# Selective scan on one core: later step-input jobs, one sum moved to VectorE, sums of a section copied out a bank earlier and in runs of 16

## The reference, cut to what matters

```python
dt = softplus(dts + dt_proj_b)            # per direction and channel
def step(h, inp):
    dt_l, u_l, B_l, C_l = inp
    dA = jnp.exp(dt_l[..., None] * A)
    h = h * dA + (dt_l * u_l)[..., None] * B_l[:, :, None, :]
    y = jnp.einsum('bkdn,bkn->bkd', h, C_l)
    return (h, y)
```

## Time and profile before

| | us |
|---|---|
| median of 3 runs (10565.58 to 10573.44) | 10570.25 |
| profiled execution, its own time | 10566.93 |
| its span in the trace | 10565.1 |
| VectorE busy | 7070.9 |
| GpSimd busy | 4147.8 |
| TensorE busy | 8515.6 |
| ScalarE busy | 4478.1 |

### The profile page before, as it was taken

One profiled execution on the slowest core, in us unless ns is written; L12 is line 12 of the kernel. 1 busy time (PEld: TensorE's weight loads), 2 busy tenths in 40 slices (PEclk: granted clock), 3 DMA queues, 4 the chain that ended last, 5 costly groups with the idle time before them and its releaser, 6 DMA issues. The chain is left out here.

```text
span 10565.1 us, 129307 instructions
## 1 busy us (share of the span) xinstructions
PE 8515.6 (81%) x40748; PEld 6002.4 (57%) x40748; DVE 7070.9 (67%) x9395; ACT 4478.1 (42%) x8485; POOL 4147.8 (39%) x2787
## 2 busy tenths in 40 slices
PE   4777777777777778599999999958558988996657
PEld 2444344434444444399999999947334444443445
DVE  6999799979997999444444454432356766653446
ACT  4666566656665666322222222223214444443231
POOL 3999599959995999211111111000000000000001
PEclk8999899999998999799999999979759999997668
DMA  4555355535553555100000000031310000103000
GB/s 129 164 162 162 110 161 161 163 110 164 161 164 110 161 162 164 43 12 14 12 13 11 13 14 10 8 103 33 130 51 19 14 19 19 28 1 130 20 21 18
DMA packets 332596, 835.12 MB, mean 79 GB/s; under 512 B 35796, under 2 KB 111832, under 8 KB 318654
## 3 DMA queue, kind: packets, MB, share of 16 engines
q1 hardware_dynamic: 331910, 826.64, 25.4%
HBM read 758.85 MB, written 39.08 MB: 76 GB/s over the span
## 5 line engine op out<-in xcount | busy, mean ns | idle before, releaser
L754 POOL TENSOR_TENSOR ss_work<-ss_dtu,ss_ringb 128x768 f32<-128x768 f32 x1536 | 2755.3, 1817 | 251.8 <-POOLq L59 248.3
L618 PE MATMUL ss_ps<-ss_work,ss_ident 128*128 128x512 f32 (+1 forms) x6144 | 2276.7, 517 | 446.8 <-POOL ss_work L764 329.5
L618 PEld LDWEIGHTS ss_ps<-ss_work,ss_ident 128*128 128x128 f32 x6144 | 1221.4, 203 | 1221.8 <-issue 872.0
L738 DVE TENSOR_TENSOR_SCAN ss_work<-ss_ps,ss_last,ss_work 128x768 f32<-128x768 f32 x1024 | 1811.2, 1802 | 95.8 <-issue 42.4
L671 ACT ACTIVATE ss_ps<-ss_dt,ss_a_neg 128x768 f32<-128x768 f32 x1536 | 1376.0, 896 | 273.1 <-DVE ss_work L738 254.6
L1234 ACT ACTIVATE stu_XT<-cv_ps 128x384 fp32r<-128x384 f32 x768 | 377.1, 491 | 1789.3 <-DVE cv_ps L1281 1361.9
L723 DVE TENSOR_TENSOR ss_work<-ss_work,ss_ps 128x1152 f32<-128x1152 f32 x768 | 1019.7, 1328 | 1.2 <-ACT ss_ps L679 1.2
L2227 ACT ACTIVATE at_probs<-at_ps 128x768 f32<-128x768 f32 x864 | 694.6, 810 | 709.3 <-PE at_ps L2181 708.7
L2245 DVE TENSOR_REDUCE at_top<-at_ps 128x1 f32<-128x384 f32 x1728 | 878.8, 553 | 167.6 <-PE at_ps L2165 165.7
L1664 POOL MEMSET c_pooled<- 128x2048 f32 x2 | 3.6, 1808 | 2487.2 <-POOLq L59 2487.2
L738 DVE TENSOR_TENSOR_SCAN ss_work<-ss_ps,ss_work 128x768 f32<-128x768 f32 x512 | 879.5, 1744 | 66.3 <-issue 33.2
(11 more groups left out here) (543 smaller groups left out, 14912.5 us busy)
## 6 DMA issues: line engine op xcount, KB each, us to landing
ss_ringb<-scan_rows SPq DMA_DIRECT2D x768, 384.0 KB, 3.7
ss_ringc<-scan_rows SPq DMA_DIRECT2D x768, 384.0 KB, 3.8
c_w<-in_l_ffn_w SPq DMA_DIRECT2D x64, 1024.0 KB, 7.4
at_packs<-at_high SPq DMA_DIRECT2D x64, 288.0 KB, 5.5
cv_raw<-in_l_ffn_phi_odd SPq DMA_DIRECT2D x16, 576.5 KB, 3.6
cv_raw<-in_l_ffn_phi_even SPq DMA_DIRECT2D x16, 576.0 KB, 4.3
at_packs<-at_qk SPq DMA_DIRECT2D x32, 288.0 KB, 5.5
ff_weights<-in_l_conv_fw SPq DMA_DIRECT2D x10, 640.0 KB, 10.4
```

Source lines behind the costliest of these rows:

```text
L618: return pe.matmul(acc[:, d * WIN + a:d * WIN + e], ident[:, :], weighed[:, t % DEEP, d, a:e], start=n == 0 and e - a == 512, stop=n == NS ...
L738: dve.tensor_tensor_scan(hid[:, t % DEEP, d, ::step], decay[d][:, ::step], drive[:, t % DEEP, d, ::step], start, ALU.mult, ALU.add).then_i ...
L754: pool.tensor_tensor(drive[:, t % DEEP, d, :], dtu[:, t // NST % 2, d, :], ringb[:, t % RING, :], ALU.mult).then_inc(s["driven"], 1)
```

## The change

Input jobs run in states 4 to 9 and sum jobs in 10 to 14, which is one fewer. The sixth sum (half 1, last 256 columns) is made by VectorE in state 12 with both operands in SBUF, and a semaphore `sum_last` tells ScalarE and GpSimd. The Exp, Ln and `weigh_input` steps move back by one state, except GpSimd's second, which stays at 13. Since no job is left in state 3, TensorE issues none inside state 0. The old `y` is added in states 5 to 8. The first `summed` of a state is signalled after the first 256 columns of half 1, and `keep_sums` of half 0 waits for that one. For column windows `keep_sums` walks its operands in the other order: it writes 16 neighbouring elements at a time and reads PSUM with a step of 48.

```diff
-    INPUT_AT, SUM_AT = (3, 4, 5, 6, 7, 8), (9, 10, 11, 12, 13, 14)
+    INPUT_AT, SUM_AT = (4, 5, 6, 7, 8, 9), (10, 11, 12, 13, 14)
     JOBS = len(INPUT_AT) + len(SUM_AT)
-    EXP_AT, LOG_AT, READY_AT = (5, 8), (6, 9), (10, 13)
-    FIRST_Y, KEEP_AT = 3, (1, 2)
+    EXP_AT, LOG_AT, READY_AT, SUM_LAST_AT = (6, 9), (7, 10), (11, 13), 12
+    FIRST_Y, KEEP_AT = 5, (1, 2)
+    def kept_sums(i, d):
+
+        return kept_jobs(i, len(INPUT_AT) + min(PARTS * (d + 1), len(SUM_AT)))
...
-                if n != 1:
-                    beside(t + 2)
+                beside(t + 2)
...
                     add_weighed(t, 0, 0, 512)
-                    beside(t + 3)
                     if i:
                         pe.wait_ge(s["kept"], D2 * i)
...
-                add_weighed(t, 0, 512, WIN).then_inc(s["summed"], 1)
-                add_weighed(t, 1, 0, 256)
+                add_weighed(t, 0, 512, WIN)
+                add_weighed(t, 1, 0, 256).then_inc(s["summed"], 1)
                 add_weighed(t, 1, 256, WIN).then_inc(s["summed"], 1)
...
-                    act.wait_ge(s["z_kept"], kept_jobs(i, len(INPUT_AT) + PARTS * (d + 1)))
+                    act.wait_ge(s["z_kept"], kept_sums(i, d))
+                    if d:
+                        act.wait_ge(s["sum_last"], i)
...
-                act.wait_ge(s["summed"], 2 * NST * (i + 1))
-                act.activation(window(y[:, d, :], SECTIONS[i]), acc[:, d * WIN:(d + 1) * WIN].rearrange("p (a b) -> p a b", b=48), ACT.Copy).then_inc(s["kept"], 1)
+                act.wait_ge(s["summed"], 2 * NST * (i + 1) - 1 + d)
+                order = "p a b -> p a b" if SECTIONS[i][0] % 2 == 0 else "p a b -> p b a"
+                total = acc[:, d * WIN:(d + 1) * WIN].rearrange("p (a b) -> p a b", b=48)
+                act.activation(window(y[:, d, :], SECTIONS[i]).rearrange(order), total.rearrange(order), ACT.Copy).then_inc(s["kept"], 1)
...
                     if d == 0 and t:
                         weigh(t - 1)
+                    if d == 0 and n == SUM_LAST_AT and i + 1 < len(SECTIONS):
+                        dve.wait_ge(s["soft"], D2 * (i + 1) + 2)
+                        z = dt[:, (i + 1) % 2, 1, WIN - SIDE:WIN]
+                        dve.tensor_tensor(z, z, dtu[:, (i + 1) % 2, 1, WIN - SIDE:WIN], ALU.add).then_inc(s["sum_last"], 1)
...
-                pool.wait_ge(s["z_kept"], kept_jobs(i, len(INPUT_AT) + PARTS * (d + 1)))
+                pool.wait_ge(s["z_kept"], kept_sums(i, d))
+                if d:
+                    pool.wait_ge(s["sum_last"], i)
```

More of the change, by code:

```diff
@@ L300, in selective_scan_mixer @@
         s1 = Signals(nc, "ss1", "loaded framed projected padded cleared conv_own conv_done convolved gated zed zgated made even_kept odd_kept")
-        s2 = Signals(nc, "ss2", "b0 b1 b2 b3 c0 c1 c2 c3 first_stored even_stored odd_stored kept_x copied driven decayed scanned weighted pool_weighted ended summed kept z_full z_kept exponent soft added dt_ready")
+        s2 = Signals(nc, "ss2", "b0 b1 b2 b3 c0 c1 c2 c3 first_stored even_stored odd_stored kept_x copied driven decayed scanned weighted pool_weighted ended summed kept z_full z_kept sum_last exponent soft added dt_ready")
         s3 = Signals(nc, "ss3", "mean centred squared varied logged sd_ready normed gated summed added stored")
```

## The result

| | us | ratio to before (95%) |
|---|---|---|
| before, 9 runs | 10570.14 (10561.05 to 10580.5) | |
| changed, 9 runs | 10593.87 (10576.19 to 10606.2) | 1.0022 (1.0012 to 1.0033) |

The change makes the kernel 24 us slower (0.22%), about the smallest difference that these runs can tell from none; 49 us less were forecast, and the range ended at 10560. All medians here are of fast runs: one run of add_11 (11086 us, granted clock 0.75 where the others have 0.91) and one of pool_add_608 (28937 us, 0.56) are left out.

The account below looks back on a forecast made before the run. VectorE was taken to bound, GpSimd close behind: 74.3 + 0.43 + 1.1 + 0.9 = 76.7 us a section, taken as 76.8 against 77.85. With 1.7 at the scan's end, 49 us for four images: 10521 us, range 10494 to 10560.

Parts of the forecast that it names:

- What bounds the kernel: Scan stage: VectorE paces, standing still some 3.5 us a section in states 2 to 4; GpSimd has 1.95 us to spare.
- Half 0 a bank sooner: Section start: ScalarE's copy of half 0 starts 0.9 us sooner, so VectorE's 1.41 us wait falls to 0.5.
- no job in state 0: Section start: TensorE goes on 1.4 us sooner, so the 1.85 us wait before state 4 becomes about 0.45.
- runs of 16: `keep_sums` of column windows: 0.8 us a copy, 0.7 saved, on VectorE's path in 5 of 11 starts.
- rival 4: GpSimd alone bounds, the addition waits little: 75.9 to 76.3 us a section, 10484 to 10500 us; chance 0.12.
- Rival 2: Column copies: the stepped PSUM read is slow; gain gone at 1.8 us a copy, 10627 at 3.0; chance 0.07.
- rival 3: TensorE's 14 restart records stay slow, the wait before state 4 stays near 1.85 us: 10563 us; chance 0.06.
- The last piece by VectorE: State 12: the addition takes 0.43 us plus a wait for GpSimd's instruction, between 0 and 2.0, taken as 1.1.
- What stays of VectorE's waits: Of VectorE's 3.5 us of waits a section, 2.6 are removed and 0.9 stays.
- the later jobs: Input jobs and GpSimd's first `weigh_input` moved later: TensorE freer in state 3, the `weigh_input` move costs nothing.
- GpSimd's share: State 12: GpSimd waits out VectorE's addition and pays 0.43 us a section, 75.9 becoming 76.3.
- Rival 1: State 12: the addition always meets a fresh `weigh_input` or drive, 2.0 + 0.43 us: 10554 to 10570; chance 0.20.

Follow-up runs that it names:

- add_11: Changed kernel with VectorE's addition in state 11 in place of 12; 10594.36 us, 1.0024 of before.
- pool_add_608: Changed kernel with the addition done by GpSimd and 608 columns of each half weighed by VectorE (576 before); 10501.76 us, 0.9936 of before.
- no_add: Changed kernel without the addition and without `sum_last`, the sixth sum left out; 10491.75 us, 0.9925 of before.
- psum_add: Changed kernel with the addition's first input taken from PSUM, so these 256 columns get another value; 10490.65 us, 0.9922 of before.
- pool_add: Changed kernel with the same addition done by GpSimd behind its weighing of state 12; 10518.18 us, 0.9949 of before.
- add_later: Changed kernel with VectorE's addition behind the scan of half 1 of state 12; 10661.26 us, 1.0086 of before.
- jobs_only: Kernel before with the later jobs alone, copies as before and no sixth sum; 10528.57 us, 0.9964 of before.
- runs16: Kernel before with only the other operand order in `keep_sums` of column windows; 10542.42 us, 0.9973 of before.
- early_keep: Kernel before with the column copies' new order and half 0's sums signalled and copied one product sooner; 10523.75 us, 0.9956 of before.

## Why the prediction was wrong

- *What bounds the kernel.* Right: GpSimd had little to spare, 1.95 us a section by the prediction's count, and with VectorE's waits gone it bounds (no_add, psum_add, pool_add).
- *Half 0 a bank sooner, no job in state 0, runs of 16.* Right in mechanism and near in size. Over the ten sections of four images 2.6 us a section make 104 us of waits to be removed; in states 2 to 4 of sections 1 to 11 107 us went. The unseen form, a PSUM read with a step, took 0.79 us as assumed. The three are worth 79 us with nothing against them; the prediction's rival 4, 10484 to 10500, is in effect its sum for them without the addition, and they came to 10492. Rival 2 was wrong, the copies do not pass 0.81 us, and the penalty that its second paragraph expects of a stepped read does not show. Of rival 3 a part came: a slower restart goes with the 0.6 us more that the wait before state 4 kept. Its own sum was wrong too: 78.1 us a section is more than the 77.85 of before, so it gives about 10573, not 10563.
- *The last piece by VectorE.* This step failed. It said that VectorE waits out GpSimd's instruction, "between 0 and 2.0 us", with 1.1 taken, which no row shows. It read one pair of rows as a rule: there the addition got in behind the one instruction that ran. The same trace holds 15 more such meetings in that layer (L1264, 2.28 to 2.30 us beside a median of 0.69), and in all of them one instruction was waited for, so the rows of before gave no warning. The runs showed that the addition may be passed by all that GpSimd has ready: it took up to 6.2 us here and 8.6 in add_later. The mean is 2.66 us, not 1.53; 44 x 1.13 = 50 us of the 73 that the forecast missed by are this difference.
- *What stays of VectorE's waits.* The sum left 0.9 us a section for them and had nothing for waits in later states. In sections 1 to 11 the changed kernel has 11.6 us in state 8, 8.8 in state 11 and 11.2 in state 14. Those of state 14 belong to the addition: there no_add and psum_add have none and add_later has 13.6. Those of state 11 belong to the later jobs, which the sum had at nothing: jobs_only has 9.9 us there, runs16 and early_keep none. Those of state 8 (2.5 and 0.8 us in no_add and psum_add, 8.5 in jobs_only) no run settles. Some 28 us more idle time outside states 2 to 4 and section 0 than before, beside the 50, cover the 73.
- *GpSimd's share* was put too high: it was to pay 0.43 us a section. Where an addition got in between two drives, the second took 0.2 us longer than its mean (3.75 us for the pair above, where others take 3.57).
- *Rival 1* named the right place, the right mechanism and the wrong limit: its bound of one instruction gave 10554 to 10570. The price per section that would have turned the sign was in no row, and I took the longest wait that a single row allowed as the worst case.
- The Trainium skill ("SBUF — State Buffer", section "Who interferes with whom") says that the loser blocks for the whole instruction. The trace agrees as far as that goes, since the additions end 0.28 us behind a GpSimd instruction, and psum_add shows that it takes the second SBUF input. The runs go beyond it, since the loser can block for several.

## What to carry to other kernels

An operation moved to VectorE with both inputs in SBUF has no fixed price beside a busy GpSimd: it may have to stand until GpSimd's own queue pauses, and all that waits for VectorE stands with it. Take one input from PSUM, or leave the operation to GpSimd, where these 44 took 32.2 us and cost 27.5. And before a small job is given to another engine, measure the rest of the change without it: here that rest was the whole gain.

## What the runs showed of the hardware that was not expected

- A 256-column addition took 0.42 us with one input in PSUM, all 44 times, and 0.41 to 6.2 us at the same place with both in SBUF.
- Which additions get in at the next boundary stays open, and the time left of GpSimd's instruction alone does not decide it. In the changed kernel 16 came with 0.35 to 0.37 us left of `weigh_input` and got in behind it (0.63 to 0.65 us in all); in add_later four came with 0.28 to 0.36 us left of it and did not. In add_later 21 came with at most 0.54 us left of a drive and got in; in add_11 nine came with 0.10 to 0.49 us left of a pair's first drive, and each waited out the second too (2.1 to 2.5 us in all). Of 13 that came within 0.1 us of a first drive's start in the changed kernel, 12 waited out that drive only (2.0 to 2.1 us). What decides this no run here was made to show.
- ScalarE reads PSUM with a step of 192 bytes in 0.79 us per 768 elements, as without a step, while the write with such a step cost 1.48.
